# First product of a fused feed-forward network moved beside the last items of the attention ahead of it

## The reference, cut to what matters

```python
def _L1_attn_ref(x, W_Q, W_K, W_V, W_O):            # 16 heads of 16, causal
    Q = x @ W_Q.T
    K = x @ W_K.T
    V = x @ W_V.T
    ...
    attn = jnp.einsum('bhqd,bhkd->bhqk', Q, K) * scale
    attn = jnp.where(causal, attn, jnp.asarray(-jnp.inf, dtype=attn.dtype))
    probs = jax.nn.softmax(attn, axis=-1)
    y = jnp.einsum('bhqk,bhkd->bhqd', probs, V)
    ...
    return y @ W_O.T

def _L1_ffn_ref(x, k0, k1, k2, s0, s1, s2):          # booleans k become +1 and -1
    h = jnp.concatenate([x, -x], axis=-1)
    h = s0 * _conn_dense(k0, h);  h = jax.nn.relu(h) * 2     # 512 -> 1024
    h = s1 * _conn_dense(k1, h);  h = jax.nn.relu(h) * 2     # 1024 -> 1024
    h = s2 * _conn_dense(k2, h)                              # 1024 -> 256
    return h

x = x + _L1_attn_ref(_layernorm(x, axis=-1), ...)
x = x + _L1_ffn_ref(_layernorm(x, axis=-1), ...)
```

## Time and profile before

| | |
|---|---|
| timed, median of 3 | 1133.53 us (1133.38 to 1135.79) |
| profiled execution, own time | 1136.18 us |
| its span, first to last instruction | 1134.5 us |
| mean granted TensorE clock | 0.941 of full |
| TensorE busy | 1044.4 us (92%) |
| VectorE busy | 640.9 us (56%) |
| ScalarE busy | 471.5 us (42%) |
| GpSimd busy | 241.8 us (21%) |

### The profile page before, as it was taken

How to read it: one execution, slowest core, us unless ns; L and a number is a source line. 1 busy time by engine, 2 the same in 40 slices (tenths; PEclk the granted TensorE clock), 3 DMA queues, 4 the chain that set the end, 5 groups by cost and what they waited for, 6 DMA issues and landing times.

```text
span 1134.5 us, 27536 instructions
## 1 busy us (share of the span) xinstructions
PE 1044.4 (92%) x11715; PEld 899.5 (79%) x11715; DVE 640.9 (56%) x1376; ACT 471.5 (42%) x865; POOL 241.8 (21%) x381
## 2 busy tenths in 40 slices
PE   3999999999998899999399999987999999997998
PEld 3788888888887778887299999975878788875887
DVE  3754645545234355765579999935666643334342
ACT  1433333333334555642156777623343342435241
POOL 2212211211211024433323444423100000010000
PEclk9899999999999799997599999987999998976999
DMA  9200000000001600220227567331110002000000
GB/s 306 92 20 20 1 20 20 1 1 1 1 1 53 274 2 3 81 90 21 68 85 264 198 201 244 132 112 47 37 32 21 2 2 67 3 2 1 1 19 19
DMA packets 55672, 72.79 MB, mean 64 GB/s; under 512 B 8504, under 2 KB 48896, under 8 KB 54912
## 3 DMA queue, kind: packets, MB, share of 16 engines
q1 hardware_dynamic: 54016, 66.85, 17.7%
q0 software_dynamic: 1536, 4.20, 1.1%
HBM read 60.02 MB, written 11.01 MB: 63 GB/s over the span
## 4 chain that ended last, share of the span: by engine, by line
PE 81%; DVE 9%; ACT 4%; issue 3%; POOL 1%; DMA 1%; SPq 0%; DVEq 0%; ACTq 0%; POOLq 0%
PE ps L600 8%; PE ps L615 8%; PE ps L2043 6%; PE ps L2059 6%; PE ps L2307 5%; PE ps L1426 4%; PE ps L632 3%; PE ps L1074 3%; PE ps L554 3%; PE ps L652 3%; PE ps L1344 2%; PE ps L1383 2%; PE ps L584 2%; PE ps L1443 2%; PE ps L1010 2%
## 5 line engine op out<-in xcount | busy, mean ns | idle before, releaser
L369 POOL TENSOR_TENSOR rn_tmp<-rn_cur,eps 128x1 f32<-128x1 f32 x48 | 13.7, 286 | 430.6 <-DVE rn_cur L363 430.5
L728 ACT ACTIVATE x0pT<-ps 128x512 f32<-128x512 f32 x64 | 38.3, 598 | 135.7 <-PE ps L615 135.7
L2043 PE MATMUL ps<-moe_xT_hi,ew_1hi 128*128 128x256 f32 x240 | 69.6, 290 | 2.3 <-DVE moe_xT_lo L2183 2.3
L2059 PE MATMUL ps<-ew_2hi,eh_hi 128*128 128x256 f32 x240 | 69.5, 289 | 2.4 <-DVE eh_lo L2191 2.4
L2189 DVE CAST eh_hi<-eh 128x512 fp32r<-128x512 f32 x60 | 61.1, 1018 | 13.8 <-ACT eh L2103 13.8
L2043 PE MATMUL ps<-moe_xT_lo,ew_1hi 128*128 128x256 f32 x240 | 68.9, 287 | 0.0
L2043 PE MATMUL ps<-moe_xT_hi,ew_1lo 128*128 128x256 f32 x240 | 68.8, 287 | 0.0
L2059 PE MATMUL ps<-ew_2hi,eh_lo 128*128 128x256 f32 x240 | 67.1, 280 | 0.0
L2059 PE MATMUL ps<-ew_2lo,eh_hi 128*128 128x256 f32 x240 | 67.0, 279 | 0.0
L2307 PE MATMUL ps<-f,ffw 128*128 128x512 f32 x256 | 59.4, 391 | 0.3 <-DVE f L2378 0.3
L907 POOL TENSOR_SCALAR x0pT<-x0pT 128x512 f32<-128x512 f32 x64 | 39.3, 614 | 87.7 <-ACT x0pT L728 85.3
(11 more groups left out here) (324 smaller groups left out, 2842.3 us busy)
## 6 DMA issues: line engine op xcount, KB each, us to landing
ew<-L_ffn_W_dram SPq DMA_DIRECT2D x30, 1024.0 KB, 7.3
x0cin<-ctx_dram SPq DMA_DIRECT2D x8, 512.0 KB, 4.2
x1cin<-ctx_dram SPq DMA_DIRECT2D x8, 512.0 KB, 4.0
xg<-moe_in SPq DMA_DIRECT2D x15, 256.0 KB, 7.7
moe_out<-moe_y SPq DMA_DIRECT2D x15, 256.0 KB, 7.8
moe_in<-padneg SPq DMA_DIRECT2D x3, 1024.0 KB, 12.3
maskrow<-mask_BxS_ik_dram SPq DMA_DIRECT2D x2, 1024.0 KB, 7.7
x0wq<-L_xattn_Wq_dram SPq DMA_DIRECT2D x1, 1024.0 KB, 7.5
```

Source lines behind the costliest of these rows:

```text
L728: nc.scalar.activation(g.pT[:, u, :], ps[:, S_BANK[u % 2], :], ACT.Exp, scale=64.0 ** -0.5).then_inc(C0.exp, 1)
L2043: last = nc.tensor.matmul(ps[:, n % 3, j * BT:j * BT + BT], w[b % 2][:, i, f * P:f * P + P], v[b % 2][:, i, :], start=(i == 0 and m == 0), ...
L2059: last = nc.tensor.matmul(ps[:, O_BANK[b % 2] + c, 0:D], v[n % 3][:, j * BT + c * P:j * BT + c * P + P], w[b % 2][:, f, :], start=(f == 0 ...
```

## The change

The norm, transposes and splitting of tiles 0 to 3 move into pass 21 of the self-attention, and the eight parts of the first product of c = 0 into passes 22 (f = 0, 1, 2), 23 (3, 4, 5) and 24 (6, 7). They become fills of the ring, `(("ff", t), "T")` and `(("ff", f), "h")`, so the bank of each comes from the common order. ScalarE's relus and VectorE's splits of them stand in the passes too. The weights are converted earlier: `ffw0` in passes 18 and 19, `ffw1` and `ffw2` two pairs per pass in passes 18 to 21. `f0` changes place in memory with the raw bytes, which now lie over `f1` alone. The products that stay use banks 2 to 5 as before and wait for the ring's last use of banks 2 and 3. Cut to its core; the hunks are, in this order, the memory, the list `FILLS`, then the loops of `pe_self`, of `act_self` (its first new block behind `neg(n)`) and of `dve_self` (its last new lines behind `residual(n - 1)`):

```diff
+        f0 = [sb(f"f0_{i}", [P, FT, 512], F32R) for i in range(2)]
         raw_at = at[0]
-        f0 = [sb(f"f0_{i}", [P, FT, 512], F32R) for i in range(2)]
...
+                if _lo and _n >= _hi - 3:
+                    if _n == _hi - 3:
+                        FILLS += _at(_n + 2, "k") + _ff("T", 0, 1) + _at(_n + 2, "q") + _at(_n - 1, "pv") + _at(_n + 2, "v") + _at(_n - 1, "T", "y") + _ff("T", 2, 3)
+                    else:
+                        f = 3 * (_n - _hi + 2)
+                        FILLS += _ff("h", f, f + 1) + _at(_n - 1, "pv") + _ff("h", *range(f + 2, min(f + 3, FT))) + _at(_n - 1, "T", "y")
+                    continue
...
+                if span == 1 and n >= hi - 3:
+                    f = 3 * (n - hi + 2)
+                    if ahead:
+                        scores(n + 1)
+                    if n == hi - 3:
+                        fill_qk(n + 2, "k")
+                        ff_rows(pe, 0)
+                        ff_rows(pe, 1)
+                        fill_pv(n - 1, 0)
+                        fill_qk(n + 2, "q")
+                        fill_pv(n - 1, 1)
+                        fill_v(n + 2)
+                    else:
+                        ff_hidden(pe, f)
+                        fill_pv(n - 1, 0)
+                        ff_hidden(pe, f + 1)
+                        fill_pv(n - 1, 1)
+                        if f + 2 < FT:
+                            ff_hidden(pe, f + 2)
+                    fill_T(n - 1)
+                    if here:
+                        exponents(n)
+                    fill_y(n - 1)
+                    if n == hi - 3:
+                        ff_rows(pe, 2)
+                        ff_rows(pe, 3)
+                    continue
...
+                if span == 1 and n == hi - 3:
+                    ff_upper(act, 0)
+                    ff_upper(act, 1)
+                if span == 1 and n > hi - 3:
+                    f = 3 * (n - hi + 2)
+                    for i in range(f, min(f + 3, FT)):
+                        ff_relu(act, i)
...
-                if span == 1 and n > lo + 1:
-                    act_ff_weights(act, n - 2 - lo)
-                if n == hi and span == 1:
-                    act_ff_weights(act, FT - 1)
+                if span == 1 and n == hi - 3:
+                    ff_upper(act, 2)
+                    ff_upper(act, 3)
+                if span == 1 and lo + 2 <= n < lo + 6:
+                    for i in range(2):
+                        act_ff_weights(act, 2 * (n - lo - 2) + i)
...
+                if span == 1 and n == hi - 3:
+                    ff_norm(dve, 0)
+                    ff_norm(dve, 1)
                 if ahead:
                     maximum(n + 1)
+                if span == 1 and n > hi - 3:
+                    ff_split(dve, 3 * (n - hi + 2))
...
+                if span == 1 and n == hi - 3:
+                    ff_lower(dve, 0)
+                    ff_lower(dve, 1)
                 if back:
                     attend(n - 1)
+                if span == 1 and n == hi - 3:
+                    ff_norm(dve, 2)
+                    ff_norm(dve, 3)
+                if span == 1 and n > hi - 3:
+                    f = 3 * (n - hi + 2)
+                    for i in range(f + 1, min(f + 3, FT)):
+                        ff_split(dve, i)
...
-                if span == 1 and n in (lo + 4, lo + 6):
-                    dve_ff_weights(dve, (n - lo - 4) // 2)
+                if span == 1 and n == hi - 3:
+                    ff_lower(dve, 2)
+                    ff_lower(dve, 3)
+                if span == 1 and n in (lo + 2, lo + 3):
+                    dve_ff_weights(dve, n - lo - 2)
```

The new helpers do what the old ones in `pe_ff`, `act_ff` and `dve_ff` did, with the ring's waits:

```diff
+        def ff_hidden(pe, f):
+            if f == 0:
+                pe.wait_ge(FF.w0, KD)
+                for t in range(4):
+                    RS.wait_emptied(pe, ("ff", t), "T")
+            RS.wait_free(pe, ("ff", f), "h")
+            for k in range(KD):
+                for part in range(2):
+                    last = nc.tensor.matmul(RS.bank(("ff", f), "h"), ffw0[:, k, f * P:f * P + P], fxT[part][:, k, :],
+                                            start=(k == 0 and part == 0), stop=(k == KD - 1 and part == 1))
+            last.then_inc(SA.fill, 1)
+
+        def ff_relu(act, f):
+            if f == 0:
+                act.wait_ge(FF.scale, 2)
+            RS.wait_filled(act, ("ff", f), "h")
+            act.wait_ge(FF.h_free, f + 1)
+            nc.scalar.activation(fh[f % 2][:, :], RS.bank(("ff", f), "h"), ACT.Relu, scale=ffs[:, 0:1]).then_inc(SA.by_act, 1)
+            if f % 2 == 1:
+                RS.wait_emptied(act, ("ff", f), "h")
+                nc.scalar.activation(f0[0][:, f, :], fh[1][:, :], ACT.Copy).then_inc(FF.hi_odd, 1)
+
+        def ff_split(dve, f):
+            if f % 2 == 0:
+                RS.wait_emptied(dve, ("ff", f), "h")
+                nc.vector.tensor_copy(f0[0][:, f, :], fh[0][:, :]).then_inc(FF.hi, 1)
+            ff_split_lower(dve, f, f0, f)
+
+        FF_LAYERS = ((0, 1), (1, 0), (1, 1))
```

More of the change, by code:

```diff
@@ L505, in build @@
         _more = [(n, "v") for n, (k, _) in enumerate(ITEMS) if k == "mla"] + [(n, k) for n, k in FILLS if k[0] == "A"]
+        _more += [(("ff", t), "T") for t in range(4)]
         _more += [(("x1", t), k) for t in range(T) for k in ("cT0", "q", "k1")]
@@ L509, in build @@
         QS = ps[:, 4:8, :]
+        last_fill = [max(n for n in range(len(FILLS)) if n % 4 == i) for i in range(4)]
         def bank_of(t, k):
@@ L2279, in act_ff_weights @@
             nc.scalar.activation(ffw2[:, one, :], raw2[:, one, :], ACT.Identity, bias=minus1[:, :], scale=2.0).then_inc(FF.w, 1)
-        def pe_ff(pe):
[L2283 to L2290, removed]
-            pe.wait_ge(FF.w, 2 * FT)
[L2292 to L2309, removed]
@@ new lines, in ff_split_lower @@
+        def ff_split_lower(dve, n, dst, f):
+            if f % 2 == 0:
+                dve.wait_ge(FF.hi, n // 2 + 1)
+            else:
+                dve.wait_ge(FF.hi_odd, n // 2 + 1)
+            nc.vector.tensor_tensor(dst[1][:, f, :], fh[f % 2][:, :], dst[0][:, f, :].bitcast(F32), ALU.subtract).then_inc(FF.split, 1)
+            dve.wait_ge(FF.split, n + 1)
+            dve.sem_inc(FF.h_free, 1)
+        FF_LAYERS = ((0, 1), (1, 0), (1, 1))
+        def pe_ff(pe):
+            pe.wait_ge(FF.w, 2 * FT)
+            for c, layer in FF_LAYERS:
+                if c == 1 and layer == 0:
+                    pe.wait_ge(FF.xT, 4)
+                w, src, ks = ((ffw0, fxT, KD), (ffw1, f0, FT))[layer]
+                for f in range(FT):
+                    n = 16 * c + 8 * layer + f
+                    if c == 0 and f in (0, 4):
+                        ff_rows(pe, 4 + f // 2)
+                        ff_rows(pe, 5 + f // 2)
+                    if n < FT + 2:
+                        RS.wait_emptied(pe, *FILLS[last_fill[2 + f]])
+                    elif n > FT + 3:
+                        pe.wait_ge(FF.r_free, n - FT - 3)
+                    for k in range(ks):
+                        if layer == 1 and f == 0:
+                            pe.wait_ge(FF.split, 16 * c + k + 1)
+                        for part in range(2):
+                            last = nc.tensor.matmul(ps[:, 2 + f % 4, :], w[:, k, f * P:f * P + P], src[part][:, k, :],
+                                                    start=(k == 0 and part == 0), stop=(k == ks - 1 and part == 1))
+                    last.then_inc(FF.r_ps, 1)
+                if layer == 0:
+                    continue
@@ L2320, in act_ff @@
         def act_ff(act):
[L2321 to L2342, removed]
@@ L2344, in dve_ff @@
-        def dve_ff(dve):
[L2345 to L2387, removed]
@@ new lines, in act_ff @@
+            for c, layer in FF_LAYERS:
+                dst = (f0, f1)[layer]
+                for f in range(FT):
+                    n = 16 * c + 8 * layer + f
+                    if c == 0 and f in (0, 4):
+                        ff_upper(act, 4 + f // 2)
+                        ff_upper(act, 5 + f // 2)
+                    act.wait_ge(FF.r_ps, n - FT + 1)
+                    act.wait_ge(FF.h_free, n + 1)
+                    nc.scalar.activation(fh[f % 2][:, :], ps[:, 2 + f % 4, :], ACT.Relu, scale=ffs[:, layer:layer + 1]).then_inc(FF.r_free, 1)
+                    if f % 2 == 1:
+                        act.wait_ge(FF.r_free, n - FT + 1)
+                        nc.scalar.activation(dst[0][:, f, :], fh[1][:, :], ACT.Copy).then_inc(FF.hi_odd, 1)
```

58 lines of the change are left out of this document (added).

## The result

The changed kernel takes 1124.93 us, median of 9 (1119.51 to 1130.37), the kernel before beside it 1134.41 us, median of 9 (1133.38 to 1139.34): ratio 0.9924 (0.9897 to 0.9951). It is faster by 9.5 to 10.9 us, under 1%, where 15.3 were forecast, and its time lies above the range's end of 1122.8.

What follows compares the result with a forecast made beforehand. TensorE was taken to lose 18.5 us before the second product and some 34 us at half clock; starting that product 17.9 us earlier, less 2.6 for a clock fall, gives 15.3 less: 1118.2 us, range 1114.4 to 1122.8.

Steps and rivals of the forecast that it cites:

- 0.9 us of transposes: Pass 21: TensorE gets the transposes of four tiles, 0.22 us each, so the pass ends at 1002.8.
- it costs nothing: Pass 21: attend of item 20 behind two lower parts is covered by TensorE's work; uncovered, up to 0.8 us.
- L: Stretch from pass 21's start to the span's end: 142.4 us before the change, forecast 127.1.
- the clock fell twice in the kernel before: Trace reading: falls in cross-attention's pv (936 to 938) and near 1006 in pass 22, TensorE busy with small matmuls alone.
- the slow rival: Clock falls in pass 22 and stays down: 1136.4 us; chance 0.05 together with no effect.
- The Trainium skill's rule named there: A kernel cycling through PSUM banks has its clock go down and up between matmul groups; would give 1136.4 us.
- the product: Passes 22 to 24: each moved part, four matmuls, takes 0.93 us of TensorE at full clock.
- The first product's wait for the last lower part: Pass 22: the first moved part waits for tile 3's lower part until 1004.9, 0.35 us after the scores.
- the waits for attend and `attT` in pass 24: Pass 24: nothing covers attend, 0.8 us, and y waits 0.5 us for `attT`; the pass takes 6.6 us.
- The fall at the end: Clock falls between 1025 and 1029.9: 2.1 us in the second product, 0.5 in transposes, together 2.6; chance 0.50.
- The gap between y and the transposes: After pass 24: near 1.9 us between the last y and tile 4's transposes, before the second product.
- Queues or an earlier fall: Relu and split delay passes, 1119.5 to 1122.5 us, or the clock falls in pass 23, 1129.1; chance 0.18.

Runs made afterwards that it cites:

- the gap put back: The change with tiles 0 and 1's transposes behind pv in pass 21, plus a TensorE wait for the keys' copy before pv: 1121.86 us, ratio 0.9890.
- both repairs: The change with tiles 0 and 1's transposes behind pv in pass 21 and tiles 4 and 5's norms and transposes in pass 24: 1114.71 us, ratio 0.9826.

## Why the prediction was wrong

*Pass 21: the step that failed.* The prediction's sum has nothing for this pass beyond 0.9 us of transposes (its "it costs nothing" is said of attend alone), and takes full clock there without a word. It walked the queues of ScalarE and VectorE, but of the ring only the waits in pass 22; the fill four places ahead of pv in the new list was never looked up. Measured in the change: 15.4 us instead of 10.8, of which 0.8 is the gap and the rest, 3.8, half clock. With the keys copied first the same pass takes 10.8, the forecast's figure (10.6 with the transposes behind pv, where the last 0.17 us of wait are gone too). This is 4.6 of the 5.2 us by which L was missed, in two of three profiles; in the third, with a short fall, 2.3.

*A reading that hid it.* The prediction says that the clock fell twice in the kernel before "at times when TensorE was busy". Near 1006 this is wrong. TensorE's last pv of pass 22 ended at 1005.80 and the next instruction is

```profile
1006.59 0.69 PE L1435 MATMUL ps<-cst,sa_att 128*128 128x128 f32 x2 [0.82 <-DVE sa_att L1721]
```

The window that holds the end of pv is

```profile
1004.00:1006.00 2.00, 1.78 (x62) 1.68 (x58) 1.62 (x4) 0.00 (x0) 0.41 (x1) 0.98 0.04 8
```

With 0.98 there and 0.50 from 1006 on, the clock fell at about 1005.9, within this gap of 0.82 us behind scores and pv. The trace of before thus had a short gap behind small matmuls with a fall beside it, which was a reason to look for such gaps in the new order.

*What brings the fall.* Shown: with the transposes ahead of pv and a gap of 0.7 to 0.8 us behind them, five of six profiles fell (the change three times, tiles 4 and 5 in pass 24 once, norms in pass 20 once of twice); with the gap alone none of four; with the transposes and a wait of only 0.17 us none of two; with neither none of four. So taking the ring's wait away, in either of two ways, took the fall away in all six profiles, and a wait of 1.12 us did not bring it back without the transposes ahead of pv. Why the two together bring it is open. They add up to a stretch without dense matmuls between the keys and the queries, and its length sorts the profiles as well: from the start of the keys to the start of the queries it is 3.41 us in the four that had the change's pass 21 (all fell), 3.30 to 3.33 in six (norms in pass 20 and the gap put back; one fell), 2.80 and 2.13 in the other six (none fell). The runs don't tell whether the kind of work counts or this length alone.

*Pass 22 to 24.* No new fall in passes 22 and 23, as forecast, so the slow rival did not come about. The Trainium skill's rule named there (TensorE: Matmul & The Clock Gate, "A second HAM failure mode: psum-queue depth-cycling") did not decide either: the kernel with both repairs cycles through the same four banks, with two fills more than the change, and holds 1.00 from pass 21 on. What fits the rule is pass 21 of the change, where a wait of 0.78 us for a bank stands ahead of the fall. A term that was mis-sized is the product: 1.13 us behind small matmuls, not 0.93; six of the eight stand so, 1.2 us. The first product's wait for the last lower part, 0.35, was 0.30 to 0.33, and nothing in the three profiles whose pass 21 took 15.4 us; the waits for attend and `attT` in pass 24, 0.8 and 0.5, were 0.82 and 0.47.

*The tail.* The fall at the end came as forecast, in all three profiles of the change, for about 7 us from near the last y. Its cost in the second product was put at 2.1; from that product's start to the end the change took 87.9 and 87.4 us against 86.9, so 0.5 to 1.0; the fall had begun before y ended, so it was over some 3 us into the product, and 0.5 of it went into y instead (1.60 for 1.06). The gap between y and the transposes, 1.9 forecast, is 1.83.

*The sum.* 142.4 - 15.3 = 127.1 forecast; 4.6 for pass 21 and about 1.2 for the products, less some 0.7 in the tail, make 132.2, and 132.3 was measured. These terms are read from rows of different profiles, so that they meet within 0.1 is partly luck. Without the fault in pass 21 the change gives L = 128.7 (keys first), 13.7 less than before, where 15.3 were forecast.

*Rivals.* "Queues or an earlier fall" (1119.5 to 1129.1, chance 0.18) is what happened, but two passes earlier than the fall that I priced (at the start of pass 23) and by way of the ring, not of relu and split; that the time lies within its bounds is no merit of its mechanism. It should have had more chance: pass 21, shown without a gap in the trace of before, was counted as safe, and nothing was weighed of what a new gap does to the clock.

## What to carry to other kernels

When fills are put into a ring of banks, write the new order down and look up for each fill, old ones too, which fill it now follows in its bank and which engine empties that one; here pv came to wait for a copy that it has nothing to do with, behind a maximum. Price a new short stall not only at its length but also at what the clock may do behind it: 0.8 us became 4.6 here, while the 1.12 us put back elsewhere stayed 1.2. And where executions scatter by 5 us for reasons upstream, compare the stretch from the last common event to the end, in several profiles.

## What the runs showed of the hardware

In pass 21 of the change TensorE's clock fell although the engine was busy 14.6 of 15.4 us there and its longest wait was 0.78 us; four times a wait of 1.12 us in the same pass, with the two transposes behind pv, left it at 1.00. When it falls, the time at half clock differs from one execution of the same kernel to the next: 3.4 us and some 10 us for the change. The kernel before scattered more widely still beside the last variants (13 executions, one of 1121.08 us, the others from 1131.27 to 1139.41), and pass 21 of the study's kernels started at 986.6 to 995.0 us with all but the same work ahead of it. A product of four 128x512 matmuls costs 1.13 us behind matmuls of 64x64 or 32-row tiles and 0.93 behind the output product's full ones.
